# An audio tower's last transfers: one per position with 32 batches outermost, and half of the last twelve issued by ScalarE

## The chip, the cores and the metric

The kernel runs on one core of a Trainium2 chip. A core has five engines with a program each: TensorE (PE in the rows) for matrix products, with its weight loads shown apart as PEld; VectorE (DVE); ScalarE (ACT); GpSimd (POOL); and SyncE (SP), which in this kernel issues the DMAs. The data of a DMA is moved by 16 DMA engines that the core's queues share. The engines and the DMAs are kept in order by semaphores; a DMA adds 16 to its semaphore when it has landed.

The metric is the device time of one execution in microseconds, the median of several. The times of before are 336.95, 337.02 and 338.04 us, so the median is 337.02 us.

## The reference

Inputs are x (64 batches, 750 samples) and weights, all in float32. Overlapping windows of 128 samples at a stride of 64 give 10 positions per batch; each is projected to 512 features. Then comes one transformer layer, with attention and a gated feed-forward network, and the output has shape (64, 10, 512).

```python
patches = x[:, idx, :].reshape(B, starts.shape[0], P * F)
h = einsum('bnp,dp->bnd', patches, W) + b               # tokens: 64 x 10 x 512
h = h + attn(layernorm(h))    # 16 heads, rope, causal scores, heavy keys and a band, softmax, Wo
gate, up = split(layernorm(h) @ w_gate_up.T, 2)         # 2 x 2048
h = h + (silu(gate) * up) @ w_down.T                    # the output
```

## The kernel before, in words

The 640 tokens are cut into five tiles of 128 (NT = 5). A tile is not a run of rows of the output: it is four quadrants of 32 SBUF partitions (GB = 32, NQ = 4), and each quadrant holds one position for 32 batches, one of the two groups of batches. The table QUADRANTS (L46) says which: tile 0 holds positions 0 to 3 of group 0, tile 1 positions 4 to 7 of group 0, tile 2 positions 8 and 9 of both groups, tiles 3 and 4 positions 0 to 3 and 4 to 7 of group 1.

Each product is made of three matmuls (mm3, L198 to L202) on operands split into a high part (made by ScalarE, L476) and a low part (made by VectorE or GpSimd). So most rows of TensorE have line L201.

The feed-forward network runs twice over its 16 blocks of 128 inner features: pass A for tiles 0 and 1, pass Z for tiles 2, 3 and 4. Each block's weights, 768 KB, are loaded by SyncE into one of four slots of the tile stage. In pass A these are L341 and L302; for pass Z the first four blocks are loaded at the end of pass A (L343 to L346), and the rest in the loop at L349 to L354, each when the low parts of the block four places before have been made (semaphores wgu_lo, wd_lo). ScalarE copies a block out of the stage (hi_gu, L519), VectorE makes the low part of gate and up (L832), GpSimd that of down (L363), and TensorE multiplies.

The order on SyncE around the change is thus: the loads of pass Z's first four blocks; tile_out for tiles 0 and 1; the loop that loads the other twelve blocks; tile_out for tiles 2, 3 and 4; and a wait for all transfers of the output (L358). tile_out (L304) waits until VectorE has added a tile's feed-forward sum to h and written it to the buffer ob (tile_sum, L861, the add is L866), and then issues one DMA for each group of batches that the tile holds. Tiles 0, 1, 3 and 4 take one DMA each, of four positions; tile 2 takes two, of two positions each. So the output takes NT + 1 = 6 DMAs. Their destination is written in the order position, batch, feature (`"b i n -> i b n"`), with the positions outermost. In pass Z VectorE waits on the semaphore dma_out before it writes a buffer of ob that pass A's transfers read.

The core ends when every engine has come to the end of its program, SyncE after its wait for dma_out.

Of the kernel before, what the change touches and what calls it, by code (L numbers as in the profile page):

```python
# [29 lines left out]
NT = TOK // P  # L30
D, H, HD = 512, 16, 32
KT = D // P
NG, GB, NQ = 2, 32, 4
# [12 lines left out]
QUADRANTS = [[(0, n) for n in range(0, 4)], [(0, n) for n in range(4, 8)],  # L46
             [(g, n) for g in range(2) for n in (8, 9)],
             [(1, n) for n in range(0, 4)], [(1, n) for n in range(4, 8)]]
# [28 lines left out]
A, Z = 0, 1  # L77
FIRST, TILES = (0, 2), (2, 3)
# [17 lines left out]
def audio_tower(nc, patches, w_tok, b_tok, w_k, w_q, w_v, w_o, w_ffn, consts, regroup, out):  # L96
    ctx = ExitStack()
    with ctx:
        def sb(name, shape, dt=F32, stack=ctx):
            return stack.enter_context(nc.sbuf_tensor(name, shape, dt))  # L100

        def sem(name):
            return ctx.enter_context(nc.semaphore(name))
# [9 lines left out]
        for name, width in CUTS.items():  # L113
# [19 lines left out]
        ob = sb("ob", [P, 3, D])  # L133
# [39 lines left out]
        dma_out = sem("dma_out")  # L173
# [14 lines left out]
        wgu_hi, wgu_lo, wd_hi, wd_lo, gu_mm, silu_done, gu_prod, hT_hi, hT_lo, down_mm, out_sb = (  # L188
            [sem(f"{n}_{p}") for p in "ab"] for n in
            ("wgu_hi", "wgu_lo", "wd_hi", "wd_lo", "gu_mm", "silu_done", "gu_prod", "hT_hi", "hT_lo", "down_mm", "out_sb"))  # L190
# [33 lines left out]
        def kq_split(eng, x, k):  # L224

            if x == 1 and k >= KT - 2:
                eng.wait_ge(wkq_lo[1], KT - 2)
                eng.wait_ge(wq_lo_late, k - (KT - 3))
            else:
                eng.wait_ge(wkq_lo[x], k + 1)  # L230
# [17 lines left out]
        def stage_count(p, i, slot):  # L248

            before = 1 + p * NB // SLOTS  # L250
            return i * (16 // SLOTS) + (16 * (before + 1) - slot * (16 // SLOTS))

        block = ctx.enter_context(nc.Block())

        @block.sync
        def _(sp):
            sp.dma_start(pat_raw[:, :], patches).then_inc(dma_pat, 16)
            sp.dma_start(wtok_raw[:, :], w_tok).then_inc(dma_tok, 16)
            sp.dma_start(bias_raw[:, :], b_tok.broadcast_to([2 * BR, D])).then_inc(dma_bias, 16)
            sp.dma_start(stage[:, 0, :], w_k).then_inc(dma_stage[0], 16)  # L260
            sp.dma_start(const[:, :], consts).then_inc(dma_const, 16)
            sp.dma_start(stage[:, 1, :], w_q).then_inc(dma_stage[1], 16)
            sp.dma_start(stage[:, 2, :], w_v).then_inc(dma_stage[2], 16)
            sp.dma_start(stage[:, 3, :], w_o).then_inc(dma_stage[3], 16)

            def leave(x, t, buffer, done):

                for q, (g, i) in enumerate(QUADRANTS[t]):
                    sp.dma_start(regroup["kqv".index(x), g, :, :, i, :].rearrange("h b n -> b h n"),  # L269
                                 buffer[GB * q:GB * (q + 1)].rearrange("p (h n) -> p h n", h=NQ)).then_inc(done, 16)  # L270

            def enter(x, t, g, done):

                dst = {"k": k_all, "q": q_all, "v": v_all}[x]
                own = [i for group, i in QUADRANTS[t] if group == g]
                at = slice(own[0], own[-1] + 1)
                sp.dma_start(dst[:, g, at, :], regroup["kqv".index(x), g].rearrange("h b i n -> (h b) i n")[:, at, :])\
                  .then_inc(done, 16)

            def pair(t):  # L280

                items = [ROTATE.index((x, t)) for x in "kq"]
                for n in items:
                    sp.wait_ge(rot_sum, n + 1)
                    leave(ROTATE[n][0], t, rot[:, n % ROT], rot_gone[n % ROT])
                for n in items:
                    sp.wait_ge(rot_gone[n % ROT], 64 * (n // ROT + 1))
                    for g in sorted({g for g, _ in QUADRANTS[t]}):
                        enter(ROTATE[n][0], t, g, dma_kq[t])

            def value_out(t):
                sp.wait_ge(v_sb, t + 1)
                leave("v", t, v_out[:, t % 2], v_gone[t % 2])

            def value_in(t):
                sp.wait_ge(v_gone[t % 2], 64 * (t // 2 + 1))
                for g in sorted({g for g, _ in QUADRANTS[t]}):
                    enter("v", t, g, dma_v[g])

            def block_load(i):  # L300
                slot = i % SLOTS
                sp.dma_start(stage[:, slot, 0:FW], w_ffn[i]).then_inc(dma_stage[slot], 16)  # L302

            def tile_out(p, u):  # L304
                sp.wait_ge(out_sb[p], u + 1)
                t = FIRST[p] + u
                for g in sorted({g for g, _ in QUADRANTS[t]}):
                    own = [(q, i) for q, (group, i) in enumerate(QUADRANTS[t]) if group == g]
                    (q0, i0), (q1, i1) = own[0], own[-1]
                    sp.dma_start(out[GB * g:GB * (g + 1), i0:i1 + 1, :].rearrange("b i n -> i b n"),  # L310
                                 ob[GB * q0:GB * (q1 + 1), u, :]).then_inc(dma_out, 16)

            pair(0)
            pair(1)

            for x in range(2):
                kq_split(sp, x, KT - 1)
                block_load(x)
            pair(2)
            value_out(0)  # L320
            value_out(1)
            value_in(0)
            value_in(1)
            value_out(2)
            value_in(2)
            sp.wait_ge(wvo_lo, KT)
            block_load(2)
            value_out(3)
            value_in(3)
            value_out(4)  # L330
            value_in(4)
            sp.wait_ge(wvo_lo, 2 * KT)
            block_load(3)
            pair(3)
            pair(4)

            with sp.Fori(0, NB // SLOTS - 1) as n:
                for u in range(SLOTS):
                    sp.wait_ge(wgu_lo[A], SLOTS * n + (u + 1))
                    sp.wait_ge(wd_lo[A], SLOTS * n + (u + 1))  # L340
                    sp.dma_start(stage[:, u, 0:FW], w_ffn[bass.ds(SLOTS * n + (SLOTS + u), 1)].rearrange("o p n -> (o p) n"))\  # L341
                      .then_inc(dma_stage[u], 16)
            for i in range(SLOTS):  # L343
                sp.wait_ge(wgu_lo[A], NB - SLOTS + i + 1)
                sp.wait_ge(wd_lo[A], NB - SLOTS + i + 1)
                block_load(i)  # L346
            for u in range(TILES[A]):
                tile_out(A, u)
            with sp.Fori(0, NB // SLOTS - 1) as n:  # L349
                for u in range(SLOTS):  # L350
                    sp.wait_ge(wgu_lo[Z], SLOTS * n + (u + 1))
                    sp.wait_ge(wd_lo[Z], SLOTS * n + (u + 1))
                    sp.dma_start(stage[:, u, 0:FW], w_ffn[bass.ds(SLOTS * n + (SLOTS + u), 1)].rearrange("o p n -> (o p) n"))\
                      .then_inc(dma_stage[u], 16)  # L354

            for u in range(TILES[Z]):
                tile_out(Z, u)
            sp.wait_ge(dma_out, 16 * (NT + 1))  # L358

        @block.gpsimd  # L360
        def _(pool):
# [112 lines left out]
        def _(act):  # L474
# [157 lines left out]
            ffn_step(Z, NB - 2, 2, next_gu=False)  # L632
            ffn_step(Z, NB - 1, 3, next_gu=False, next_down=False)

        @block.vector
        def _(dve):
            steps = [0]
# [223 lines left out]
            def tile_sum(p, u):  # L861

                dve.wait_ge(down_mm[p], NB + u)
                if p == Z and u < TILES[A]:
                    dve.wait_ge(dma_out, 16 * TILES[A])
                dve.tensor_tensor(ob[:, u], ps[:, DOWN[p][u], :], h[:, FIRST[p] + u], ALU.add).then_inc(out_sb[p], 1)  # L866


# [56 lines left out]
            for u in range(TILES[A]):  # L925
                tile_sum(A, u)
# [8 lines left out]
            for u in range(TILES[Z]):  # L935
                tile_sum(Z, u)
# [229 lines left out]
```

## Time and profile before

| what | value |
| --- | --- |
| median of three executions | 337.02 us (336.95 to 338.04) |
| span of the profiled execution, first to last instruction | 334.9 us |
| what the median has beyond that span | 2.1 us |
| the profiled execution's own time | not stated by the page; taken as its span and the 2.1 us |
| TensorE busy | 280.9 us (84%) |
| VectorE busy | 210.3 us (63%) |
| GpSimd busy | 157.8 us (47%) |
| ScalarE busy | 111.8 us (33%) |
| time of the packets of SyncE's DMA queue, share of 16 engines | 37.3% |
| mean granted TensorE clock | 0.946 of full |

The span is cut into 40 slices in the page, so a slice is 8.4 us. TensorE is at nine tenths or more in nearly all slices of the second half until the last two, which read 3 and 0; in the same two slices the DMA moves 24 and 70 GB/s. A busy share is a mean over stages with different limits; what a stage's edit is worth has to be read at its place.

### The profile page before, as it was taken

The numbers are of one execution on the slowest core, as the hardware profiler recorded it, in microseconds if no ns is written. First come the engines' busy times: TensorE is split into PE (matmuls) and PEld (weight loads), VectorE is DVE, ScalarE is ACT, GpSimd is POOL, SyncE is SP. The second block draws the span as 40 slices with busy tenths as digits, with TensorE's granted clock in tenths as the row PEclk, the third lists the DMA queues.
The fourth block names the chain that finished last, engine by engine and source line by source line (L and its number), as shares of the span: only waits on it lengthen the run. The fifth ranks groups of instructions, "written<-read, shape, count | busy, mean of one in ns | idle before, by whom it ended". The sixth has DMA issues, their size and how long they took to land.

```text
span 334.9 us, 4376 instructions
## 1 busy us (share of the span) xinstructions
PE 280.9 (84%) x1528; PEld 247.4 (74%) x1528; DVE 210.3 (63%) x307; ACT 111.8 (33%) x185; POOL 157.8 (47%) x107
## 2 busy tenths in 40 slices
PE   2889689957696898949579998999999999999930
PEld 1468468847585797848469997889999999999920
DVE  4687999999569998598599266554342342342130
ACT  3650110072001544543821033344443443443200
POOL 0656784147847599574599005614223223223100
PEclk9999979989787899989979999999999999999995
DMA  7904777427442054433222202326442433410002
GB/s 251 389 0 95 203 246 179 127 46 206 104 119 94 2 190 145 156 136 125 94 94 94 96 0 80 105 100 225 154 156 94 143 139 94 140 48 0 0 24 70
DMA packets 17602, 39.89 MB, mean 119 GB/s; under 512 B 1908, under 2 KB 10356, under 8 KB 17076
## 3 DMA queue, kind: packets, MB, share of 16 engines
q1 hardware_dynamic: 17588, 39.71, 37.3%
q8 instruction: 7, 0.11, 0.1%
q14 instruction: 7, 0.06, 0.1%
HBM read 34.46 MB, written 5.24 MB: 119 GB/s over the span
## 4 chain that ended last, share of the span: by engine, by line
PE 46%; DVE 28%; issue 9%; ACT 4%; DMA 4%; POOL 3%; SPq 2%; DVEq 0%; ACTq 0%; POOLq 0%
PE ps L201 40%; DVE prod L236 5%; PE ps L1008 4%; DVE hT L847 3%; DVE sm L701 3%; DVE xn L664 2%; POOL wvo L363 2%; DVE pr L729 2%; DVE rstd L661 2%; DVE gu L841 1%; SPq L269 1%; DMA bias_raw<-b_tok 1%; DVE prod L240 1%; DMA regroup<-rot 1%; DVE xT L671 1%
## 5 line engine op out<-in xcount | busy, mean ns | idle before, releaser
L201 PE MATMUL ps<-xT,wgu 128*128 128x256 f32 (+1 forms) x768 | 123.6, 319 | 1.9 <-DVE xT L671 1.8
L201 PEld LDWEIGHTS ps<-xT,wgu 128*128 128x128 f32 x768 | 120.6, 197 | 5.3 <-DVE xT L671 2.5
L363 POOL TENSOR_TENSOR wd<-stage,wd 128x512 fp32r<-128x512 f32 x32 | 52.1, 1631 | 79.2 <-ACT wd L476 79.2
L201 PE MATMUL ps<-wd,hT 128*128 128x512 f32 x240 | 62.7, 403 | 14.6 <-DVE hT L847 13.2
L201 PEld LDWEIGHTS ps<-wd,hT 128*128 128x128 f32 x240 | 44.3, 190 | 24.2 <-DVE hT L847 14.7
L841 DVE TENSOR_TENSOR gu<-silu,ps 128x256 f32<-128x256 f32 (+1 forms) x32 | 15.5, 484 | 62.1 <-PE ps L201 44.2
L363 POOL TENSOR_TENSOR wgu<-stage,wgu 128x1024 fp32r<-128x1024 f32 x16 | 40.0, 2498 | 13.3 <-ACT wgu L476 13.3
L476 ACT ACTIVATE wgu<-stage 128x1024 fp32r<-128x1024 f32 x32 | 33.7, 1055 | 22.8 <-PE ps L201 20.3
L201 PE MATMUL ps<-wvo,xT 128*128 128x512 f32 x120 | 33.6, 439 | 5.1 <-issue 3.2
L847 DVE TENSOR_TENSOR hT<-gu,hT 128x256 fp32r<-128x256 f32 (+1 forms) x32 | 24.3, 759 | 20.5 <-ACT hT L476 20.5
L201 PEld LDWEIGHTS ps<-wvo,xT 128*128 128x128 f32 x120 | 25.2, 215 | 11.9 <-issue 3.3
L1008 PE MATMUL ps<-const,prod 128*128 128x128 f32 x220 | 27.6, 287 | 5.8 <-DVE prod L240 5.8
L1008 PEld LDWEIGHTS ps<-const,prod 128*128 128x128 f32 x220 | 27.0, 202 | 7.0 <-issue 6.2
L577 ACT ACTIVATE silu<-ps 128x256 f32<-128x256 f32 (+1 forms) x32 | 14.0, 436 | 48.7 <-PE ps L201 48.7
L476 ACT ACTIVATE xT<-ps 128x512 fp32r<-128x512 f32 (+1 forms) x16 | 9.1, 572 | 57.2 <-PE ps L1008 29.6
L476 ACT ACTIVATE hT<-gu 128x256 fp32r<-128x256 f32 (+1 forms) x32 | 14.8, 462 | 35.1 <-DVE gu L841 35.0
L240 DVE TENSOR_TENSOR prod<-v_all,pr 128x896 f32<-128x896 f32 (+8 forms) x15 | 25.9, 1766 | 0.1
L476 ACT ACTIVATE wd<-stage 128x512 fp32r<-128x512 f32 x32 | 20.0, 624 | 8.1 <-PE ps L201 8.1
L236 DVE TENSOR_TENSOR prod<-q_all,k_all 128x128 f32<-128x128 f32 (+7 forms) x15 | 21.5, 1435 | 0.0
L386 POOL TENSOR_TENSOR rot<-rot_cos,rot_sin 128x512 f32<-128x512 f32 x10 | 12.8, 1283 | 17.5 <-DVE rot_sin L692 17.5
L832 DVE TENSOR_TENSOR wgu<-stage,wgu 128x1024 fp32r<-128x1024 f32 x16 | 19.7, 1234 | 1.0 <-ACT wgu L476 1.0
L377 POOL TENSOR_SCALAR var<-mv 128x1 f32<-128x1 f32 x10 | 2.4, 238 | 33.9 <-DVE mv L653 33.9
(76 smaller groups left out, 270.8 us busy)
## 6 DMA issues: line engine op xcount, KB each, us to landing
stage<-w_ffn SPq DMA_DIRECT2D x32, 768.0 KB, 4.3
regroup<-rot SPq DMA_DIRECT2D x40, 64.0 KB, 2.4
regroup<-v_out SPq DMA_DIRECT2D x20, 64.0 KB, 1.9
stage<-w_k SPq DMA_DIRECT2D x1, 1024.0 KB, 6.4
stage<-w_q SPq DMA_DIRECT2D x1, 1024.0 KB, 8.9
stage<-w_v SPq DMA_DIRECT2D x1, 1024.0 KB, 10.9
stage<-w_o SPq DMA_DIRECT2D x1, 1024.0 KB, 12.9
k_all<-regroup SPq DMA_DIRECT2D x4, 256.0 KB, 2.8
```

What stands on the lines that cost most here:

```text
L201: ins = pe.matmul(dst, lhs[a], rhs[b], start=first and n == 0, stop=last and n == 2)
L236: return eng.tensor_tensor(products(i), repeated(q_all[:, g, i], 1, i + 1), k_all[:, g, 0:i + 1], ALU.mult)
L240: return eng.tensor_tensor(products(i).rearrange("p j (h d) -> p j h d", d=HD), v_all[:, g, 0:i + 1].rearrange("p j (h d) -> p j h d", d=H ...
L363: pool.tensor_tensor(dst, src, f32(hi), ALU.subtract).then_inc(done, 1)
L386: pool.tensor_tensor(rot[:, n % ROT], rot_cos[:, n % 2], rot_sin[:, n % 2], ALU.add).then_inc(rot_sum, 1)
L476: act.activation(dst, src, ACT.Copy).then_inc(done, 1)
L577: act.activation(silu[:, ring, cols], ps[:, gate, at:at + P * TILES[p]], ACT.Silu).then_inc(silu_done[p], 1)
L701: dve.tensor_reduce(sm[:, i, :, 0:i + 1].rearrange("p h j -> p j h"), products(i).rearrange("p j (h d) -> p j h d", d=HD), AX_X, ALU.add). ...
L832: dve.tensor_tensor(wgu[:, ring, 1], stage[:, slot, 0:2 * KT * P], f32(wgu[:, ring, 0]), ALU.subtract)\
L841: dve.tensor_tensor(gu[:, ring, cols], silu[:, ring, cols], ps[:, up, at:at + P * TILES[p]], ALU.mult)\
L847: dve.tensor_tensor(hT[:, ring, 1, cols], gu[:, ring, cols], f32(hT[:, ring, 0, cols]), ALU.subtract).then_inc(hT_lo[p], 1)
L1008: ins = pe.matmul(dst, products(i)[:, j], cut["ident"], start=j == 0, stop=j == i)
```

## The change

The helper store issues the DMA of one quadrant: 32 batches, one position, 512 features, 64 KB, with the batches outermost in the destination. A tile takes four of them, so the output takes 20 DMAs in place of six. SyncE issues all four of tiles 0 and 1. Of tiles 2, 3 and 4 it issues quadrants 0 and 1 (partitions 0 to 63), and ScalarE issues quadrants 2 and 3 at the end of its program, behind its last feed-forward step. The counts that are waited for on dma_out follow.

```diff
+        def store(eng, t, q, buffer):
+
+            g, i = QUADRANTS[t][q]
+            eng.dma_start(out[GB * g:GB * (g + 1), i, :], ob[GB * q:GB * (q + 1), buffer, :]).then_inc(dma_out, 16)
+
...
-            def tile_out(p, u):
+            def tile_out(p, u, quarters):
                 sp.wait_ge(out_sb[p], u + 1)
-                t = FIRST[p] + u
-                for g in sorted({g for g, _ in QUADRANTS[t]}):
-                    own = [(q, i) for q, (group, i) in enumerate(QUADRANTS[t]) if group == g]
-                    (q0, i0), (q1, i1) = own[0], own[-1]
-                    sp.dma_start(out[GB * g:GB * (g + 1), i0:i1 + 1, :].rearrange("b i n -> i b n"),
-                                 ob[GB * q0:GB * (q1 + 1), u, :]).then_inc(dma_out, 16)
+                for q in quarters:
+                    store(sp, FIRST[p] + u, q, u)
...
             for u in range(TILES[A]):
-                tile_out(A, u)
+                tile_out(A, u, range(NQ))
...
             for u in range(TILES[Z]):
-                tile_out(Z, u)
-            sp.wait_ge(dma_out, 16 * (NT + 1))
+                tile_out(Z, u, range(NQ // 2))
+            sp.wait_ge(dma_out, 16 * NQ * NT)
...
+            for u in range(TILES[Z]):
+                act.wait_ge(out_sb[Z], u + 1)
+                for q in range(NQ // 2, NQ):
+                    store(act, FIRST[Z] + u, q, u)
+
...
                 if p == Z and u < TILES[A]:
-                    dve.wait_ge(dma_out, 16 * TILES[A])
+                    dve.wait_ge(dma_out, 16 * NQ * TILES[A])
```

The end of SyncE's program before, from the loop over the last twelve weight blocks on; out_sb_b is the semaphore of pass Z's finished tiles:

```order
L349 REGISTER_ALU
L349 COMPARE_AND_BRANCH
L310 DMA out<-ob 2x32x512 [waits out_sb_b]
L310 DMA out<-ob 2x32x512
L310 DMA out<-ob 4x32x512 [waits out_sb_b] x2
L98 UNCONDITIONAL_BRANCH [waits dma_out]
```

And the same place now:

```order
L350 COMPARE_AND_BRANCH
L256 DMA out<-ob 32x512 [waits out_sb_b]
L256 DMA out<-ob 32x512
L256 DMA out<-ob 32x512 [waits out_sb_b]
L256 DMA out<-ob 32x512
L256 DMA out<-ob 32x512 [waits out_sb_b]
L256 DMA out<-ob 32x512
L98 UNCONDITIONAL_BRANCH [waits dma_out]
```

SyncE issues six DMAs of 64 KB where it issued four of 128 and 256 KB; the outermost count of each is 32 where it was 2 or 4.

The end of ScalarE's program now, from its last step of the feed-forward network; before, it ended with the row of hT:

```order
L578 ACTIVATE silu<-ps 128x384 [waits gu_mm_b]
L477 ACTIVATE hT<-gu 128x384 [waits down_mm_b,gu_prod_b]
L256 DMA out<-ob 32x512 [waits out_sb_b]
L256 DMA out<-ob 32x512
L256 DMA out<-ob 32x512 [waits out_sb_b]
L256 DMA out<-ob 32x512
L256 DMA out<-ob 32x512 [waits out_sb_b]
L256 DMA out<-ob 32x512
L98 UNCONDITIONAL_BRANCH
```

Nothing else of ScalarE stands behind the six new DMAs.

In the middle of SyncE's program, where the first two tiles leave, there is now:

```order
L307 DMA stage<-w_ffn 128x1536 [waits wd_lo_a,wgu_lo_a] x4
L256 DMA out<-ob 32x512 [waits out_sb_a]
L256 DMA out<-ob 32x512 x3
L256 DMA out<-ob 32x512 [waits out_sb_a]
L256 DMA out<-ob 32x512 x3
L350 UNCONDITIONAL_BRANCH
L350 ISA
L354 ISA [waits wd_lo_b,wgu_lo_b]
L354 DMA stage<-w_ffn 128x1536
```

Eight DMAs of the output stand here in place of two, ahead of the load of pass Z's fifth block.

## Rows read from the trace of the kernel before

**Rows 1.** The page of before: head line, four of its parts.

```profile
span 334.9 us, 4376 instructions
...
PE 280.9 (84%) x1528; PEld 247.4 (74%) x1528; DVE 210.3 (63%) x307; ACT 111.8 (33%) x185; POOL 157.8 (47%) x107
...
q1 hardware_dynamic: 17588, 39.71, 37.3%
...
PE 46%; DVE 28%; issue 9%; ACT 4%; DMA 4%; POOL 3%; SPq 2%; DVEq 0%; ACTq 0%; POOLq 0%
```

**Rows 2.** The chain of waits, its last three pieces: start us, us, what.

```profile
216.95 1.38 PE ps L201 x6
218.74 102.04 PE ps L201 x531
320.80 1.37 DVE ob L866 x2
```

**Rows 3.** Waits of the SP queue: us in total, times, longest us.

```profile
SPq L98 <- DMA out<-ob: 11.1, 1, 11.1
```

**Rows 4.** Timeline of the tail: start us, us, engine, line, tiles, count.

```profile
317.95 0.53 ACT L476 ACTIVATE hT<-gu 128x384 fp32r<-128x384 f32 x1 [2.21 <-DVE gu L841]
320.12 2.05 DVE L866 TENSOR_TENSOR ob<-ps,h 128x512 f32<-128x512 f32 x3 [1.06 <-PE ps L201]
320.84 0.56 SPq L310 DMA_DIRECT2D out<-ob  x1
321.45 0.53 SPq L310 DMA_DIRECT2D out<-ob  x1
322.03 0.59 SPq L310 DMA_DIRECT2D out<-ob  x1
322.66 0.81 SPq L310 DMA_DIRECT2D out<-ob  x1
```

**Rows 5.** Windows of the tail; last two columns DMA share of 16 engines, GB/s.

```profile
321.00:322.00 1.00, 0.44 (x2) 0.02 (x1) 1.00 (x2) 0.00 (x0) 0.00 (x0) 1.00 0.00 0
322.00:323.00 1.00, 0.00 (x0) 0.00 (x0) 0.17 (x1) 0.00 (x0) 0.00 (x0) 1.00 0.11 16
323.00:324.00 1.00, 0.00 (x0) 0.00 (x0) 0.00 (x0) 0.00 (x0) 0.00 (x0) 1.00 0.13 33
324.00:325.00 1.00, 0.00 (x0) 0.00 (x0) 0.00 (x0) 0.00 (x0) 0.00 (x0) 1.00 0.26 55
330.00:331.00 1.00, 0.00 (x0) 0.00 (x0) 0.00 (x0) 0.00 (x0) 0.00 (x0) 0.50 0.26 90
322.00:335.00 13.00, 0.00 (x0) 0.00 (x0) 0.17 (x1) 0.00 (x0) 0.00 (x0) 0.66 0.20 60
```

**Rows 6.** The tile v_out: its stores' issue ns min/median/max, and their landing.

```profile
L269 SPq DMA_DIRECT2D regroup<-v_out x20: 318/442/457, 49.6 to 75.5; - x20
...
DMA to landing us min/median/max: 1.7/1.9/2.6
```

**Rows 7.** Timeline of the SP queue around four stores of v_out.

```profile
74.07 1.89 SPq L269 DMA_DIRECT2D regroup<-v_out  x4
77.45 0.34 SPq L277 DMA_DIRECT2D v_all<-regroup  x1
```

**Rows 8.** Line 353, the weight loads of pass Z, in the same columns.

```profile
L353 SPq DMA_DIRECT2D stage<-w_ffn x12: 332/333/347, 226.4 to 290.5; - x12
...
DMA to landing us min/median/max: 4.2/4.3/9.6
```

**Rows 9.** Line 310, the output's transfers.

```profile
L310 SPq DMA_DIRECT2D out<-ob x6: 527/578/808, 224.7 to 322.7; - x6
```

**Rows 10.** Line 269, all stores to regroup.

```profile
L269 SPq DMA_DIRECT2D regroup<-rot x40: 303/448/1218, 26.6 to 93.3; - x40
...
DMA to landing us min/median/max: 1.6/2.2/6.2
```

**Rows 11.** Timeline around the first two tiles' transfers.

```profile
223.94 1.38 DVE L866 TENSOR_TENSOR ob<-ps,h 128x512 f32<-128x512 f32 x2 [1.88 <-PE ps L201]
224.66 1.30 SPq L310 DMA_DIRECT2D out<-ob  x2
226.39 0.35 SPq L353 DMA_DIRECT2D stage<-w_ffn  x1
227.30 2.29 POOL L363 TENSOR_TENSOR wd<-stage,wd 128x512 fp32r<-128x512 f32 x1 [6.32 <-ACT wd L476]
229.81 0.34 SPq L353 DMA_DIRECT2D stage<-w_ffn  x1
236.05 1.06 ACT L476 ACTIVATE wgu<-stage 128x1024 fp32r<-128x1024 f32 x1 [2.47 <-DMA stage<-w_ffn]
238.03 1.22 DVE L832 TENSOR_TENSOR wgu<-stage,wgu 128x1024 fp32r<-128x1024 f32 x1
243.40 0.87 PE L201 MATMUL ps<-xT,wgu 128*128 128x384 f32 x4
```

## The prediction

> **What bounds the kernel now.** I read the page first. TensorE is the busiest engine by far [rows 1], but the change touches nothing of it, so its share says only that all else has to be judged by whether TensorE, or the end of the program, waits for it. Next came the chain of waits. Its last pieces are one unbroken stretch of TensorE of 102.04 us and then VectorE's last two adds, from 320.80 to 322.17 us [rows 2]. There the chain stops, while the span goes on to 334.9 us. So 12.8 us at the end belong to no computing engine. The waits of the SP queue name them: 11.1 us at the end of the program for the landing of the output [rows 3].
>
> The timeline of the tail gives the times. The first of three adds begins at 320.12 us and takes 0.69 (2.05 for the three), so tile 2 is ready at 320.81; SyncE issues at 320.84, 321.45, 322.03 and 322.66 us, and the last issue takes 0.81, to 323.47 [rows 4]. 323.47 + 11.1 = 334.57 us is the landing, and the remaining 0.36 us are the end of the program. So what stands after the last add is: 0.5 us until the last issue, 0.8 of issue, 11.1 of landing, 0.36 of ending.
>
> Why does it take so long to land 768 KB? The windows of the tail answer. No packet moves before 322 us. Then the DMA share is 0.11 and 0.13 in the two microseconds in which only tile 2's transfers can be under way, and 0.26 later on [rows 5]. Two of sixteen engines are 0.125, four are 0.25. The destinations of these transfers have an outermost count of 2 (tile 2) and 4 (tiles 3 and 4), so I read the share as: a transfer uses as many engines as that count, and always the same first ones, since tiles 3 and 4 together do not reach above 0.26. Over the 13 us from 322 to 335 the mean share is 0.20 [rows 5], which is 0.20 x 16 x 13 = 41.6 us of one engine's work. Twelve engines or more lie idle.
>
> A rule of the Trainium skill says the same (page "DMA: Bandwidth & Descriptors", section "Why a DMA increments its semaphore by 16 and not by 1"): the engines that a transfer uses are the largest number up to 16 that divides the slowest dimension of both sides. By it the old transfers run on 2 and 4 engines, on which the shares agree, and the new ones, with 32 outermost, on 16, which no output transfer of this trace shows.
>
> **The tail, term by term.** Removed are four transfers; added are twelve of 64 KB, six on each queue. The stores of v_out have just this size, with 32 batches outermost, and show what such a transfer costs. Their issue takes 0.44 us (0.32 to 0.46) and they land 1.9 us after it (1.7 to 2.6) [rows 6]. Four in a row take 1.89 us [rows 7], so one starts every (1.89 - 0.44) / 3 = 0.48 us. The old output transfers start every 0.61 us [rows 4], and their destination has one dimension more than the new.
>
> On SyncE, then: first issue at 320.84, as now. Tile 3 is ready at 321.50 and tile 4 at 322.17, before the third and the fifth issue are due in either case, so the queue is never starved by VectorE. By the step of v_out the sixth issue starts at 320.84 + 5 x 0.48 = 323.24 and lands at 323.24 + 1.9 = 325.14. By the step of the old output transfers it starts at 323.89 and lands at 325.79. The end of the program, 0.36, makes the span 325.5 or 326.15 us.
>
> On ScalarE no DMA issue exists in the trace of before. ScalarE is free: its last operation, the split of hT, ends at 318.48 [rows 4], before VectorE's adds, and nothing stands behind its six issues. I bound its step by the rows of SyncE. The loads of pass Z, with two dimensions, take 0.33 us each [rows 8], the longest issue of the output's line 0.81 [rows 9] and the longest of the stores to regroup 1.22 us [rows 10]. By the nearest rows, the same two as above, ScalarE ends when SyncE does.
>
> The data must also fit. At the same rate per engine the 41.6 us of work are 41.6 / 16 = 2.6 us when spread evenly. Packets begin about 1.2 us after the first issue, so at 322.1 + 2.6 = 324.7 all data could have moved: before 325.1, so the issues and not the bytes set the end, though by little.
>
> I take the middle between the two steps, a span of 325.8 us. The gain is 334.9 - 325.8 = 9.1 us, and on the median 337.02 - 9.1 = **327.9 us**. The 2.1 us between span and median I leave as they are. A second queue in use could change them in either direction; nothing in the trace tells, and I give it no more than some tenths.
>
> The bounds of the tail: at best the last tile's transfers leave at once (ready 322.17, second issue 0.34 later, landing 1.7): 324.2, span 324.6, time 326.7. At worst within the rows of this line: a step of 0.81 + 0.05 gives a sixth issue at 325.14, landing 2.6 later, span 328.1, time 330.2.
>
> The Trainium skill holds a rule against this change (same page, section "Rules for kernel authors"): do not split a transfer into disjoint partition halves, since both halves run on the same 16 engines anyway, and do not spread transfers over issuing engines for bandwidth. It supposes that one transfer already fills 16 engines. Rows 5 show that it doesn't here. On the second half the rule and my sum agree: ScalarE saves only issue time, the six further steps that SyncE would otherwise take, 6 x 0.48 = 2.9 us.
>
> **The first two tiles.** Here SyncE issues eight transfers where it issued two, ahead of the load of pass Z's fifth block. Now they start at 224.66 and take 1.30 us, and the load goes out at 226.39 [rows 11]. Eight steps of 0.48 end at 228.5, and with the same 0.43 us to the loop's first load it goes out at 228.9, 2.5 us late. (By 0.86 a step it is 231.9.) The second load waits for GpSimd's part, over at 229.59, and goes out at 229.81, so it is hardly late.
>
> Who waits for that load? ScalarE, which got it at 236.05 after having waited 2.47 us, 9.66 us after its issue; the median of this line's twelve landings is 4.3 us [rows 8, 11]. I read the excess as the same defect: the 512 KB of tiles 0 and 1 sit on four engines, and the load's part on these four comes behind them. Spread over 16 engines they are gone in a quarter of the time. So the load, 2.5 us later out, lands at 228.9 + 4.3 = 233.2, or at 231.9 + 4.3 = 236.2 in the bad case: between 2.8 us earlier and no later than now. And TensorE does not feel either: the block's low part is ready at 238.03 + 1.22 = 239.25 us and TensorE comes to the block at 243.40 [rows 11], a slack of 4.15 us. I cost this part at nothing. If the cover were gone it would cost what the load is late beyond 4.15 us.
>
> VectorE's wait on dma_out before the last adds costs nothing either: these eight transfers have landed some 90 us earlier. Nor does ScalarE's new code delay anything, as it stands at the very end.
>
> **The rivals.**
>
> *ScalarE's queue is slower than SyncE's.* It was never used in the program, and its issue may cost more than the rows of SyncE. For it speaks that no row shows it; against it, only that the work is the same. With the longest issue of a regroup store, 1.22 us and 0.05 between, its sixth starts at 327.2, lands 2.6 later, span 330.2, time 332.2; with the longest landing of a regroup store, 6.2 us [rows 10], 335.9. Chance 0.11, from 330.2 us up to 336.
>
> *The change doesn't widen the transfers, or only splits them.* If the low shares had another cause, such as the memory's rate for rows of 2 KB far apart, the data would still need most of its time: with four engines evenly loaded 322.1 + 41.6 / 4 = 332.5, and with the 0.36 and the 2.1 us 335.0. This is also where the skill's rule on halves would lead if one transfer had all the engines already: the flow would stay what it is, and the two further issues on a queue would add 2 x 0.48, 338.0 us. Against both stand the steps in the share at 2/16 and 4/16. Chance 0.02 for the first and 0.01 for the second.
>
> *Slower: the small stores of one queue do not overlap.* Six on each queue, one after the other, take 6 times the landing. The point from which that is slower than now is (334.57 - 320.84) / 6 = 2.29 us each; with the longest 2.6 us the end is 320.84 + 15.6 = 336.4, and the time 338.9. Against it: the four v_out stores were issued from 74.07 on, and the load that waits for all of them went out at 77.45 [rows 7]. That is 3.4 us for four and not 4 x 1.9. Chance 0.01.
>
> *The late load stalls TensorE.* It needs an issue step far over 0.86 us in the middle too. It would give back one to three microseconds: 329 to 331. Chance 0.02.
>
> **How the numbers follow.** The forecast, 326.7 to 330.2, has a chance of 0.79, and something quicker still (a shorter end of program, quicker landing) 0.04. With the rivals this makes 1. The range holds the forecast's case and a little below it: 326.4 to 330.2 us. What this kernel's measurement can tell from no change is about 0.3%, 1 us. Faster has 0.97: all but the cases around 338 and a remainder. Within 0.3% has 0.01, slower 0.02.
>
> **What would show it.** In the profile after, the windows from 322 us on should show a DMA share well above 0.5 for some 2 to 3 us, and the SP queue's last wait should be 1.5 to 2.5 us in place of 11.1. The new issues should take 0.34 to 0.55 us each on SyncE; ScalarE's tell the first rival. The last issue of either queue should start at 323.2 to 323.9. TensorE's last stretch should stay at 102 us, and the longest landing of a weight load of pass Z should fall from 9.6 us towards 4.3 to 7. The prediction is wrong if the share stays near 0.25, if the last issues come after 325.2, or if TensorE's last stretch has a hole near 243 us.

## The result, and the profile after

The changed kernel takes 327.70 us, median of five runs (324.37 to 328.05), beside 337.14 us of the kernel before in the same comparison (336.95 to 338.04). The ratio is 0.972, with a 95% interval of 0.9671 to 0.9769. That is 9.4 us less, where 9.1 were forecast. Here and below ratios and intervals are of fast runs alone, while the medians also count four slow ones: 345.57 us in the experiment "Pairs", and 339.06, 339.76 and 933.11 us of the kernel before.

The page of the kernel after, its head and two of its parts, which answer to [rows 1]:

```profile
span 322.6 us, 4390 instructions
...
PE 278.0 (86%) x1528; PEld 244.4 (76%) x1528; DVE 209.8 (65%) x307; ACT 112.0 (35%) x185; POOL 157.7 (49%) x107
...
q1 hardware_dynamic: 17600, 39.32, 37.8%
q10 hardware_dynamic: 288, 0.39, 0.3%
```

TensorE's busy time is 278.0 us where it was 280.9, and there is a second queue, q10, which carries ScalarE's six stores. The span is 12.3 us shorter, though, and not 9.4. Two different things are in it, and the chain of waits parts them. Its last two pieces (start us, us, what), beside [rows 2]:

```profile
215.58 102.07 PE ps L201 x531
317.68 1.37 DVE ob L872 x2
```

TensorE's last stretch is as long as before, 102.07 us, but begins at 215.58 us in place of 218.74. 3.2 us were gained before the change has any place in the program; the first experiment comes to that. (The profiled execution took 324.37 us, the shortest of the five.) VectorE's last add ends at 319.05 us. The span ends at 322.6. So **3.5 us** stand behind the last add, where there were 12.8.

The timeline of that tail, for [rows 4]; SyncE's and ScalarE's stores, and SyncE's last one by itself:

```profile
316.99 2.06 DVE L872 TENSOR_TENSOR ob<-ps,h 128x512 f32<-128x512 f32 x3 [1.08 <-PE ps L201]
...
317.70 2.71 SPq L256 DMA_DIRECT2D out<-ob  x6
...
317.71 2.79 ACTq L256 DMA_DIRECT2D out<-ob  x6
...
319.98 0.43 SPq L256 DMA_DIRECT2D out<-ob  x1
```

Both queues start at 317.70 us, as soon as the first tile is there, and issue six stores in 2.71 and 2.79 us. The last wait of the SP queue, for [rows 3] (us in total, times, longest us):

```profile
SPq L98 <- DMA out<-ob: 1.8, 1, 1.8
```

11.1 us have become 1.8. The windows, for [rows 5] (the last two columns are the DMA share of 16 engines and GB/s):

```profile
318.00:319.00 1.00, 0.32 (x2) 0.00 (x0) 1.00 (x2) 0.00 (x0) 0.00 (x0) 1.00 0.40 96
319.00:320.00 1.00, 0.00 (x0) 0.00 (x0) 0.05 (x1) 0.00 (x0) 0.00 (x0) 1.00 1.01 283
320.00:321.00 1.00, 0.00 (x0) 0.00 (x0) 0.00 (x0) 0.00 (x0) 0.00 (x0) 1.00 0.97 283
321.00:322.00 1.00, 0.00 (x0) 0.00 (x0) 0.00 (x0) 0.00 (x0) 0.00 (x0) 0.98 0.42 125
```

The share was 0.11 to 0.26 for twelve microseconds; now it is about 1 for two, with 0.40 and 0.42 beside them. The sum, 2.8 us of all sixteen engines, is what the forecast had as 2.6. The stores' line (issue time in ns, minimum, median and maximum; times to landing), for [rows 6, 9]:

```profile
L256 SPq DMA_DIRECT2D out<-ob x14: 353/427/527, 221.5 to 320.0; - x14
L256 ACTq DMA_DIRECT2D out<-ob x6: 413/435/453, 317.7 to 320.1; - x6
...
DMA to landing us min/median/max: 1.7/1.8/2.1
```

ScalarE's issue costs as much as SyncE's, 0.435 and 0.427 us.

### The profile page after: what moved, and what is told of

Its sections match the earlier page's. It is cut to its first block, busy times and chain, and to the rows that moved or that the text cites. A ratio compares the mean times of both kernels' runs of the same rounds, so it can differ in the third digit from the quotient of the medians.

```text
span 322.6 us, 4390 instructions
## 1 busy us (share of the span) xinstructions
PE 278.0 (86%) x1528; PEld 244.4 (76%) x1528; DVE 209.8 (65%) x307; ACT 112.0 (35%) x185; POOL 157.7 (49%) x107
## 4 chain that ended last, share of the span: by engine, by line
PE 49%; DVE 28%; issue 9%; ACT 5%; POOL 3%; DMA 3%; SPq 2%; DVEq 0%; ACTq 0%; POOLq 0%
PE ps L201 41%; DVE prod L236 5%; PE ps L1014 4%; DVE hT L853 3%; DVE sm L707 3%; SPq L274 2%; POOL wvo L364 2%; DVE pr L735 2%; DVE gu L847 2%; DMA bias_raw<-b_tok 1%; DVE xn L670 1%; DVE prod L240 1%; DVE xT L677 1%; DVE rstd L667 1%; DVE rowv L725 1%
## 5 line engine op out<-in xcount | busy, mean ns | idle before, releaser
L201 PE MATMUL ps<-xT,wgu 128*128 128x256 f32 (+1 forms) x768 | 121.2, 314 | 1.9 <-DVE xT L677 1.8
L201 PEld LDWEIGHTS ps<-xT,wgu 128*128 128x128 f32 x768 | 118.1, 192 | 5.3 <-DVE xT L677 2.5
L201 PE MATMUL ps<-wd,hT 128*128 128x512 f32 x240 | 64.0, 409 | 15.2 <-DVE hT L853 13.6
L201 PEld LDWEIGHTS ps<-wd,hT 128*128 128x128 f32 x240 | 45.3, 195 | 25.2 <-DVE hT L853 15.0
L364 POOL TENSOR_TENSOR wgu<-stage,wgu 128x1024 fp32r<-128x1024 f32 x16 | 40.1, 2505 | 12.3 <-ACT wgu L477 12.3
L201 PE MATMUL ps<-wvo,xT 128*128 128x512 f32 x120 | 31.0, 412 | 5.7 <-issue 3.2
L201 PEld LDWEIGHTS ps<-wvo,xT 128*128 128x128 f32 x120 | 23.2, 197 | 11.8 <-POOL wvo L364 3.4
L387 POOL TENSOR_TENSOR rot<-rot_cos,rot_sin 128x512 f32<-128x512 f32 x10 | 12.8, 1284 | 17.5 <-DVE rot_sin L698 17.5
L707 DVE TENSOR_REDUCE sm<-prod 128x4 f32<-128x128 f32 (+9 forms) x20 | 17.5, 885 | 0.5
```

The source lines that it names most:

```text
L201: ins = pe.matmul(dst, lhs[a], rhs[b], start=first and n == 0, stop=last and n == 2)
L364: pool.tensor_tensor(dst, src, f32(hi), ALU.subtract).then_inc(done, 1)
L387: pool.tensor_tensor(rot[:, n % ROT], rot_cos[:, n % 2], rot_sin[:, n % 2], ALU.add).then_inc(rot_sum, 1)
L707: dve.tensor_reduce(sm[:, i, :, 0:i + 1].rearrange("p h j -> p j h"), products(i).rearrange("p j (h d) -> p j h d", d=HD), AX_X, ALU.add). ...
```

## The experiments

All figures called tail are read as above: from the end of VectorE's last add to the end of the span, in each run's profile. They are compared rather than the medians where a difference is below 2 us, for a reason that the first run shows.

**The changed kernel again.** No edit.

> The changed kernel once more, as the measure of the others of this group. The tail, from the end of VectorE's last add to the end of the span, was 3.5 us in its first profile and 12.8 before. Theory (the width of a transfer: its engines follow the outermost count): the tail is 3.5 us again, 327 to 328 us by the median. Rival (part of the gain is that this profile's TensorE clock was granted better, at 0.973): the tail stays 3.5 us, but the start of TensorE's last stretch moves between 215.5 and 219 us with the granted clock.

Measured: 328.58 us median, ratio 0.9698 (0.9652 to 0.9744). The head of the page, and then the end of the chain of waits:

```profile
span 327.1 us, 4390 instructions
```

```profile
220.12 102.04 PE ps L201 x531
322.19 1.37 DVE ob L872 x2
```

The tail is 327.1 - 323.56 = 3.5 us again. But the last stretch of TensorE begins at 220.12 us, 4.5 us later than in the first profile of the same kernel, later than in the one of before, and beyond the 219 us that were named above. So the start of that stretch varies from run to run and is no effect of the change. One place where it comes about can be seen by laying the first profiles of both kernels side by side: in the timeline 24 matmuls of the output projection, and in the windows two of their microseconds (the third column from the end is the granted clock). Before, timeline and window:

```profile
88.08 8.54 PE L201 MATMUL ps<-wvo,xT 128*128 128x512 f32 x24 [3.16 <-issue]
```

```profile
90.00:92.00 2.00, 2.00 (x6) 1.59 (x5) 0.00 (x0) 0.00 (x0) 2.00 (x2) 0.50 0.76 211
```

After, the same two views:

```profile
88.26 5.74 PE L201 MATMUL ps<-wvo,xT 128*128 128x512 f32 x24 [3.16 <-issue]
```

```profile
90.00:92.00 2.00, 2.00 (x10) 1.66 (x9) 0.69 (x1) 0.00 (x0) 2.00 (x2) 1.00 0.80 222
```

The same 24 matmuls take 8.54 us at a clock of 0.50 (the lower level, 1.2 GHz) and 5.74 us at 1.00 (2.4 GHz). In both, TensorE was at work only part of the time in the microseconds before and then waited 3.16 us. This one fall of the clock is 2.8 of the 3.2 us between the profiles of before and after. It is not the only thing that moves. In the profile of this run the 24 matmuls take 8.44 us, so the clock at this place is 2.7 of its 4.5 us; but another 1.2 us are there early on, since TensorE's first stretch of 36 matmuls begins at 24.04 us where it began at 22.80, with a granted clock of 1.00 up to there in both. What makes that part is left open.

**All twelve stores on SyncE.**

```diff
-                tile_out(Z, u, range(NQ // 2))
+                tile_out(Z, u, range(NQ))
...
-            for u in range(TILES[Z]):
-                act.wait_ge(out_sb[Z], u + 1)
-                for q in range(NQ // 2, NQ):
-                    store(act, FIRST[Z] + u, q, u)
```

> All twelve stores of the last three tiles on SyncE, none on ScalarE; still 32 batches outermost. Theory (width brings the gain, the second queue only saves issue time): the twelve start every 0.47 us from just after the first add, the last one 11 x 0.47 = 5.2 us after the first, lands 1.8 later; the tail is 3.5 + 6 x 0.47 = 6.3 us, DMA share about 0.6 in it, time 2.8 us over the changed kernel. Rival (the second queue brings the width): the tail goes back to 10 us or more.

Measured: 328.03 us, ratio 0.9708 (0.967 to 0.9746). The SP queue's stores in the timeline, then its last wait, then a window of the tail:

```profile
319.94 5.52 SPq L256 DMA_DIRECT2D out<-ob  x12
```

```profile
SPq L98 <- DMA out<-ob: 1.3, 1, 1.3
```

```profile
322.00:323.00 1.00, 0.00 (x0) 0.00 (x0) 0.00 (x0) 0.00 (x0) 0.00 (x0) 1.00 0.57 135
```

VectorE's last add ends at 321.27 and the span at 327.2, so the tail is 5.9 us: 2.4 over the changed kernel, where 2.8 were expected. The share of 0.57 shows the engines waiting for SyncE's issues, one per 0.46 us, (5.52 - 0.43) / 11. The medians don't show the 2.4 us (328.03 here, 328.58 for the changed kernel in the same comparison), since the play of some microseconds ahead of the tail lies over them; the profile does. Most of the gain, 6.9 of 9.3 us, thus needs no second queue.

**The old shape on two queues.** From the kernel before: tile 3's transfer is issued by ScalarE.

```diff
-            for u in range(TILES[Z]):
+            for u in (0, 2):
                 tile_out(Z, u)
...
+            act.wait_ge(out_sb[Z], 2)
+            wide_out(act, Z, 1)
```

(wide_out holds the issue of the old tile_out, with the engine as an argument; the diff leaves its definition out.)

> The transfers of before, positions outermost (2, 2, 4 and 4), but tile 3's issued by ScalarE, the others by SyncE; the first two tiles as before. Theory (width): the same four engines carry the same bytes, share 0.25, tail 12 to 13 us, time as before, 337 us. Rival (two queues run on different engines or double the rate): the share reaches 0.5 and the tail falls to 8 us, 332 us.

Measured: 338.57 us, ratio 1.0027 (0.9997 to 1.0057), no difference that can be told. ScalarE's issue in the timeline, then SyncE's last wait, then two windows:

```profile
319.35 1.28 ACTq L258 DMA_DIRECT2D out<-ob  x1
```

```profile
SPq L98 <- DMA out<-ob: 13.1, 1, 13.1
```

```profile
328.00:330.00 2.00, 0.00 (x0) 0.00 (x0) 0.00 (x0) 0.00 (x0) 0.00 (x0) 0.50 0.26 91
332.00:334.00 2.00, 0.00 (x0) 0.00 (x0) 0.00 (x0) 0.00 (x0) 0.00 (x0) 0.50 0.04 16
```

The share stays at 0.26 with two queues at work, so the second queue brings no engines. The tail is 334.1 - 320.0 = 14.1 us, 1.3 longer than before and longer than I expected. The last window has a share of 0.04, which is 0.04 x 16 x 2 = 1.3 us of one engine's work in those 2 us: some engine was late at the end. Why is left open; the transfers, their outermost counts and their bytes are as before. ScalarE's one issue took 1.28 us, where its stores in the changed kernel take 0.44.

**Pairs: two positions to a transfer.** From the changed kernel; each of the last three tiles leaves in one such transfer from SyncE (q = 0) and one from ScalarE (q = 2). The new issue alone is shown:

```diff
...
+            eng.dma_start(out[GB * g:GB * (g + 1), i:i + 2, :].rearrange("b i n -> i b n"),
+                          ob[GB * q:GB * (q + 2), buffer, :]).then_inc(dma_out, 16)
...
```

> Each of the last three tiles leaves in two transfers of two positions and 128 KB, one from each queue, positions outermost (2); the first two tiles as in the changed kernel. Theory (the engines used are as many as the outermost count, and always the first ones): everything runs on 2 engines, share 0.125; the work of 41.6 us on one engine takes 20.8 us on two, the tail is about 21 to 23 us, time about 346 us, slower than before. Rival (what costs is the number of bytes of a transfer, or the second queue spreads them): six transfers of 128 KB end no later than before's 12.8 us.

Measured: 343.11 us, ratio 1.0159 (1.0112 to 1.0206), slower than the kernel before by 1 to 2%, though its transfers are smaller and a second queue helps. SyncE's last wait, then a window of the tail:

```profile
SPq L98 <- DMA out<-ob: 17.4, 1, 17.4
```

```profile
328.00:330.00 2.00, 0.00 (x0) 0.00 (x0) 0.00 (x0) 0.00 (x0) 0.00 (x0) 0.50 0.13 51
```

The share is 0.13, two engines of sixteen, with both queues at work: so they use the same two. The tail is 338.6 - 320.23 = 18.4 us where I expected 21 to 23. The mechanism holds and the price was off. I had taken 41.6 us of engine time from the share of before as a fixed amount of work. But two engines move 51 GB/s here, 25.5 each, while the four of before made 90 GB/s at a share of 0.26 in [rows 5], or 22.5, and less in other windows. A nearer measure is the bytes on the busiest engine: before, if every transfer runs on the first engines, two of them serve tile 2 as well as tiles 3 and 4 and carry 128 + 64 + 64 = 256 KB and the wait is 11.1 us; here each carries 384 KB, and 11.1 x 1.5 = 16.7 us is near the 17.4 measured. It is an estimate and no more. By this count the other two engines carry 128 KB, which at 25.5 GB/s is 5 us, and yet all four were still at work 8 us after the first packets (0.26 at 330 us in [rows 5]). So the rate of an engine differs from one stage to another, and no run here shows what sets it.

**31 rows in place of 32.** The changed kernel with one number more:

```diff
-            eng.dma_start(out[GB * g:GB * (g + 1), i, :], ob[GB * q:GB * (q + 1), buffer, :]).then_inc(dma_out, 16)
+            m = 31 if t >= FIRST[Z] else GB
+            eng.dma_start(out[GB * g:GB * g + m, i, :], ob[GB * q:GB * q + m, buffer, :]).then_inc(dma_out, 16)
```

> The changed kernel, but each of the last twelve stores leaves out its last batch: 31 rows of 2 KB in place of 32, so 12 of the 640 output rows are not written. Same queues, same number of transfers, 3% fewer bytes. Theory (a transfer runs on the largest number of engines up to 16 that divides its outermost count): 31 is prime, so all twelve run on one engine, share 0.06; before, the two busiest engines moved 256 KB each in some 11.1 us, 23 KB/us; 744 KB at that rate take 32 us, the tail is 33 to 34 us, time about 358 us. Rival (the transfer takes as many engines as its outermost count allows, uneven shares permitted; or the small transfer is what helps): the tail stays 3.5 to 4 us.

Measured: 357.06 us in two executions, ratio 1.0591 (1.0548 to 1.0635), 29 us over the changed kernel for leaving out one row of 32. The head of the page, the end of the chain, and a window of the tail:

```profile
span 355.3 us, 4390 instructions
```

```profile
322.25 1.37 DVE ob L873 x2
```

```profile
330.00:340.00 10.00, 0.00 (x0) 0.00 (x0) 0.00 (x0) 0.00 (x0) 0.00 (x0) 0.50 0.07 26
```

The tail is 355.3 - 323.62 = 31.7 us, with a share of 0.07 and 26 GB/s: one engine of sixteen (0.0625). It is a little less than the 33 to 34 us expected, as the one engine moves 26 GB/s where 23 were put. Queue, number of transfers, size and the lie of the rows in memory are those of the changed kernel, to 3%. What is left is the divisor of the count. The Trainium skill states it so (page "DMA: Bandwidth & Descriptors", section "Why a DMA increments its semaphore by 16 and not by 1"): the largest number up to 16 that divides the slowest dimension of both sides, with 127 partitions on one engine as an example. This trace agrees with its 0.07.

**30 rows.** The same edit with 30.

> As the run with 31 rows, but with 30: 24 output rows are not written. Theory: 15 divides 30, so fifteen engines work, share up to 0.94, tail 3.5 us, time as the changed kernel. Rival (any count that isn't 32 or a power of two falls back to few engines): tail as with 31 rows.

Measured: 328.44 us in two executions, ratio 0.9742 (0.9685 to 0.9799). The same three views:

```profile
span 326.0 us, 4390 instructions
```

```profile
321.23 1.38 DVE ob L873 x2
```

```profile
323.00:324.00 1.00, 0.00 (x0) 0.00 (x0) 0.00 (x0) 0.00 (x0) 0.00 (x0) 1.00 0.88 266
```

The tail is 326.0 - 322.61 = 3.4 us, as with 32 rows, and the share 0.88 in the busiest microsecond: fifteen engines (0.94) would allow it, one or two would not. So 31 is bad for its divisors and not for being odd in size.

**Only the last three tiles changed.** The first two leave in one transfer each, as before. The counts that are waited for on dma_out follow; the diff leaves them out.

```diff
-                tile_out(A, u, range(NQ))
+                sp.wait_ge(out_sb[A], u + 1)
+                wide_out(sp, A, u)
```

> The last three tiles as in the changed kernel, the first two as before (one transfer of four positions each). Theory (all the gain is in the tail, the first two tiles cost and bring nothing): time as the changed kernel, 327 to 328 us; the longest landing of a weight load of pass Z is again 9 to 10 us, and ScalarE waits some 2.5 us for it, but TensorE's last stretch stays 102.1 us. Rival (the first two tiles' old transfers cost something too): the last stretch is longer than 102.1 us by what they cost.

Measured: 327.27 us, ratio 0.972 (0.9677 to 0.9763), the same as the changed kernel. The chain's end, and then the waits on a DMA between 218 and 240 us (us in total, times, longest):

```profile
218.14 102.07 PE ps L201 x531
320.24 1.38 DVE ob L881 x2
```

```profile
ACT wgu L486 <- DMA stage<-w_ffn: 2.6, 1, 2.6
```

The times to landing of pass Z's weight loads (minimum, median, maximum):

```profile
DMA to landing us min/median/max: 3.9/4.3/9.8
```

The late load is back, at 9.8 us, and ScalarE waits 2.6 us for it; TensorE's stretch is 102.07 us all the same. The tail is 3.5 us.

**Only the first two tiles changed.** The last three leave by SyncE as before, through wide_out.

> The first two tiles as in the changed kernel (eight stores), the last three as before. Theory: time as before, 337 us, tail 12.8 us; the longest landing of a weight load of pass Z is 6 to 7 us and ScalarE does not wait for it; TensorE's last stretch is 102.1 us. Rival (the six further issues on SyncE delay the weight loads so that TensorE waits, or the quicker landing helps it): that stretch differs from 102.1 us by more than 0.3.

Measured: 337.20 us, ratio 1.000 (0.9965 to 1.0035). The chain's end, and then SyncE's last wait:

```profile
219.92 102.07 PE ps L201 x531
322.01 1.37 DVE ob L876 x2
```

```profile
SPq L98 <- DMA out<-ob: 11.2, 1, 11.2
```

The times to landing of pass Z's weight loads here:

```profile
DMA to landing us min/median/max: 3.9/4.3/6.7
```

The eight stores in the middle bring nothing and cost nothing: the stretch is 102.07 us and the tail 336.4 - 323.38 = 13.0 us.

**Three queues.** GpSimd issues two of tile 2's stores, on a semaphore of its own, so that SyncE and ScalarE have five each. GpSimd's part alone is shown:

```diff
...
+            pool.wait_ge(out_sb[Z], 1)
+            for q in (1, 3):
+                store(pool, FIRST[Z], q, 0, pool_out)
...
```

> The changed kernel with two of the last twelve stores (both of tile 2) issued by GpSimd, so that SyncE and ScalarE have five each. Theory (the end is set by the last issue and its landing): both queues are free when tile 4 is ready, the last issue starts 0.5 us earlier and the tail is 3.0 us instead of 3.5, if GpSimd's two land within 4.5 us of its wait; the time is too near to the changed kernel to be told. Rival (GpSimd's queue is slow, or its first use costs): its two land last, the tail is 4 to 8 us.

Measured: 327.76 us, ratio 0.9738 (0.9694 to 0.9782). VectorE's adds and GpSimd's issues in the timeline, then SyncE's last waits: L360 of this kernel is the wait for pool_out, GpSimd's two stores, and L98 that for dma_out, the stores of the other queues:

```profile
318.41 2.05 DVE L876 TENSOR_TENSOR ob<-ps,h 128x512 f32<-128x512 f32 x3 [1.06 <-PE ps L201]
```

```profile
319.42 1.23 POOL L256 DMA_DIRECT2D out<-ob  x2 [6.00 <-DVE ob L876]
```

```profile
SPq L360 <- DMA out<-ob: 1.3, 1, 1.3
SPq L98 <- DMA out<-ob: 1.2, 1, 1.2
```

VectorE's last add ends at 320.46 and the span at 324.5, a tail of 4.0 us, where the theory said 3.0. The times to landing of GpSimd's two stores, and then of ScalarE's five, counted from the start of an issue:

```profile
DMA to landing us min/median/max: 2.4/2.6/2.7
```

```profile
DMA to landing us min/median/max: 1.9/2.7/2.9
```

GpSimd's second issue starts at 320.14 us and is in by 322.8, where SyncE's first wait ends (321.56 + 1.3). ScalarE's fifth issue starts at 321.17 and is in by 324.1, where the second wait ends. So GpSimd's stores did not land last, and the rival fails in that, though 4.0 is the low end of its range. The last issue starts 0.7 us after the last add where it was 1.0, so 0.3 us were gained; but the last landing takes 2.9 us where it took 2.1. All twelve stores share the sixteen engines, whose share is 0.96 from 321 to 322 us and 0.85 in the next; whether that or GpSimd's way of issuing made the landing longer is left open. None of the kernels that write the whole output has a shorter tail than the 3.5 us of the changed one.

## Why the prediction was right, point by point

**What bounds the kernel.** The step from the end of the chain to the span's end (12.8 us that no engine computes in) was the right place. It is 3.5 us now, and everything else of the span but the play ahead of TensorE's last stretch stands as it was.

**The width.** The reading of the shares 0.11 to 0.13 and 0.25 as 2 and 4 engines of 16 was the central step, and the runs show it from four sides: a count of 2 gives a share of 0.13, 31 gives 0.07, 30 up to 0.88, 32 about 1. That the engines are always the same first ones, also from two queues, is borne out by 0.13 with pairs and 0.26 with the old shape. The sum for the data, 2.6 us on sixteen engines, came out at 2.8. As a price for fewer engines the same 41.6 us were too much: 18.4 us of tail for pairs where 21 to 23 stood.

**The issue terms.** I had 0.48 us a step and 1.9 to landing from the stores of v_out, or 0.61 a step from the old transfers, and took the middle. Measured are 0.46 (2.71 us for six, less 0.43, over five) and a landing of 1.8 (1.7 to 2.1). The sixth issue of SyncE starts 2.28 us after its first; the forecast had 2.4 to 3.05. So the simple two-dimensional store is at the low end, and the tail 3.5 where 3.6 was forecast (325.8 - 322.17). That it is so near is in part luck: the issues took 0.4 us less than the middle that was put in, 2.72, and the last landing, 2.1 us after ScalarE's sixth issue starts, 0.2 more than the 1.9. So is the 0.2 us by which the median was missed, with executions from 324.37 to 328.05 us and a median of 328.58 when the kernel ran again.

**ScalarE's queue**, the rival with the largest chance, did not come: 0.435 us an issue. What it is worth is 2.4 us, by the run with SyncE alone; the forecast said 2.9.

**The first two tiles.** The stretch of the change after, for [rows 11]:

```profile
221.51 3.74 SPq L256 DMA_DIRECT2D out<-ob  x8
...
225.65 0.38 SPq L354 DMA_DIRECT2D stage<-w_ffn  x1
...
232.21 1.06 ACT L477 ACTIVATE wgu<-stage 128x1024 fp32r<-128x1024 f32 x1 [1.80 <-PE ps L201]
```

The stores begin at 221.51, the first load of pass Z goes out at 225.65. That is 4.14 us after the first store, where it was 1.73, so 2.4 us late against 2.5 forecast. The longest landing is

```profile
DMA to landing us min/median/max: 4.0/4.3/6.6
```

6.6 us where it was 9.6, inside the 4.3 to 7 that were named. It is now that of another load, though. The one that the forecast was about, issued at 225.65, has

```profile
DMA to landing us min/median/max: 4.5/4.5/4.5
```

4.5 us, where 4.3 was put for it. So it lands 4.14 + 4.5 = 8.6 us after the first store, where it took 1.73 + 9.66 = 11.4. ScalarE's copy of that block starts at 232.21 after a wait for TensorE alone, and no more for the DMA. That the late landing came from the old transfers was read from the trace and is now shown by the two runs with half of the change each: 9.8 us with the old ones, 6.7 with the new. And that it is worth nothing to TensorE is shown too, 102.07 us in both.

**The rivals.** "Doesn't widen" falls with the share, "small stores do not overlap" with six stores landed within 4.5 us of the first issue, "late load" with the unbroken stretch.

**What I didn't foresee** is that one profile may lie 3 us beside another by what happens ahead of the change, most of it here through the granted clock (2.8 us of 3.2). The forecast of the span, 325.8 us, was missed by 3.2 us almost for that reason alone, while 327.9 for the median was 0.2 off.

## What to carry to other kernels

Look at the DMA share in the tail as a fraction of sixteen: a share that stays at 0.06, 0.13 or 0.25 said here that the transfers ran on 1, 2 or 4 engines, with 62, 128 and 256 KB each, and the remedy is the order of its dimensions (a count with a large divisor up to 16 outermost), not another queue. A middling share can be something else: 0.57 with SyncE alone was sixteen engines waiting for the next issue. A second queue is worth the issue time that it takes over, 2.4 us for six stores here. Splitting without widening can be slower: pairs of positions on two queues took 343.11 us beside 337.39 for the old six transfers.

## What the runs showed of the hardware that was not expected

The same kernel's last TensorE stretch begins at 215.58 us in one profile and 220.12 in another; the 24 matmuls of one projection take 8.54 us at a granted clock of 0.50 and 5.74 at 1.00, and some 1.2 us of the 4.5 arise at full clock. A difference of 2.4 us is thus not to be had from five runs' medians, but from the tails of single profiles.

One row of 32 left out of each of the last twelve stores makes the tail 31.7 us in place of 3.5.

With two of twelve stores issued by GpSimd the tail is 4.0 us and not 3.5, though GpSimd's own are in 1.2 us before the last: the others then take up to 2.9 us to land, where they took up to 2.1 us with two queues.
